# A four-layer graph network on one core: GRU states through a DRAM scratch and VectorE block transposes, with a new order of steps

## What is computed

```python
x = _layernorm(x + _L0_gnn_ref(x, adj, ...))     # attention, 4 heads: "pre"
x = _layernorm(x + _L1_gnn_ref(x, adj, ...))     # 3 GRU turns: "gru"
x = _layernorm(x + _L2_gnn_ref(x, L2_adj, adj, ...))  # relations: "rel"
x = _layernorm(x + _L3_gnn_ref(x, adj, ...))     # attention, 1 head: "post"

# _L1_gnn_ref
for i in range(3):
    m = jnp.einsum('bnd,de->bne', h, weight[i])
    aggr = jnp.einsum('bst,bsd->btd', A, m)
    h = _gru_cell(aggr, h, w_ih, w_hh, b_ih, b_hh)
```

## Time and profile before

| | |
|---|---|
| median of 3 runs | 2612.03 us (2610.0 to 2612.58) |
| profiled execution | 2609.57 us, of which the span 2607.8 |
| granted TensorE clock, mean | 0.991 |
| TensorE busy | 2514.1 us, 96% |
| VectorE busy | 1962.8 us, 75% |
| ScalarE busy | 1779.6 us, 68% |
| GpSimd busy | 1240.7 us, 48% |
| DMA | 198.51 MB, 611560 packets |

### The profile page before, as it was taken

One profiled execution on the slowest core, in us unless ns is written; L12 is line 12 of the kernel. 1 busy time (PEld: TensorE's weight loads), 2 busy tenths in 40 slices (PEclk: granted clock), 3 DMA queues, 4 the chain that ended last, 5 costly groups with the idle time before them and its releaser, 6 DMA issues. The chain is left out here.

```text
span 2607.8 us, 48430 instructions
## 1 busy us (share of the span) xinstructions
PE 2514.1 (96%) x14379; PEld 2158.4 (83%) x14379; DVE 1962.8 (75%) x4883; ACT 1779.6 (68%) x4536; POOL 1240.7 (48%) x1584
## 2 busy tenths in 40 slices
PE   7999999999999999999999999999999999999985
PEld 6888888888888888888888888888888888888874
DVE  7867777777777777777777777777777777787653
ACT  6556776676776676776676776676776676776654
POOL 1344555554554544554554554444555454455442
PEclk9999999999999999999999999999999999999996
DMA  5222333333333333333333233333333333233200
GB/s 152 83 50 69 78 91 73 78 80 78 72 92 72 81 76 85 70 88 76 79 75 89 68 86 77 78 75 82 75 84 80 76 78 86 68 84 76 49 14 23
DMA packets 611560, 198.51 MB, mean 76 GB/s; under 512 B 456768, under 2 KB 596288, under 8 KB 611264
## 3 DMA queue, kind: packets, MB, share of 16 engines
q1 hardware_dynamic: 559472, 146.54, 26.2%
q10 hardware_dynamic: 51792, 48.38, 5.5%
HBM read 146.81 MB, written 48.01 MB: 75 GB/s over the span
## 5 line engine op out<-in xcount | busy, mean ns | idle before, releaser
L988 PE MATMUL psum<-ag_h,wc_h 128*128 128x512 f32 (+1 forms) x1188 | 489.3, 412 | 5.5 <-DVE ag_l L1519 3.5
L988 PE MATMUL psum<-ht_h,whh_h 128*128 128x512 f32 (+1 forms) x1188 | 476.9, 401 | 1.4 <-ACT g_z L1220 1.4
L988 PE MATMUL psum<-ht_h,whh_l 128*128 128x512 f32 (+1 forms) x1188 | 461.9, 389 | 0.0
L988 PE MATMUL psum<-ht_l,whh_h 128*128 128x512 f32 (+1 forms) x1188 | 461.9, 389 | 0.0
L988 PE MATMUL psum<-ag_h,wc_l 128*128 128x512 f32 (+1 forms) x1188 | 461.6, 389 | 0.0
L988 PE MATMUL psum<-ag_l,wc_h 128*128 128x512 f32 (+1 forms) x1188 | 461.3, 388 | 0.0
L1643 POOL TENSOR_TENSOR ht<-ht,g_n 128x512 f32<-128x512 f32 (+1 forms) x198 | 264.6, 1336 | 252.0 <-ACT g_n L1225 251.8
L1592 POOL TENSOR_SCALAR rstd<-moments 128x2 f32<-128x2 f32 x256 | 66.5, 260 | 664.7 <-DVE moments L1444 657.1
L988 PEld LDWEIGHTS psum<-ag_h,wc_h 128*128 128x128 f32 x1188 | 224.2, 189 | 57.2 <-DVE ag_l L1519 15.7
L988 PEld LDWEIGHTS psum<-ht_h,whh_l 128*128 128x128 f32 x1188 | 223.8, 188 | 50.5
L988 PEld LDWEIGHTS psum<-ag_h,wc_l 128*128 128x128 f32 x1188 | 223.5, 188 | 50.2
(11 more groups left out here) (150 smaller groups left out, 6123.0 us busy)
## 6 DMA issues: line engine op xcount, KB each, us to landing
x_kept<-x ACTq DMA_DIRECT2D x118, 256.0 KB, 2.2
x_blocks<-x_kept SPq DMA_DIRECT2D x472, 64.0 KB, 2.4
first_scores<-first_kept SPq DMA_DIRECT2D x116, 256.0 KB, 3.5
adj_i<-in_adj_dram SPq DMA_DIRECT2D x128, 128.0 KB, 3.3
x_in<-in_x_dram SPq DMA_DIRECT2D x64, 256.0 KB, 4.1
out_dram<-out_t ACTq DMA_DIRECT2D x64, 256.0 KB, 2.3
x_blocks<-in_x_dram SPq DMA_DIRECT2D x232, 64.0 KB, 3.4
part<-in_adj_dram SPq DMA_DIRECT2D x32, 256.0 KB, 3.3
```

The lines of the kernel that those rows point to most:

```text
L988: last = mm(dst, s, m, start=(first and k == 0), stop=(last_part and k == len(flat) - 1))
```

## The change

The states of layers 0 and 1 of halves 2 to 29 no longer go through TensorE and ScalarE on their way to hn. A new step h_keep, in ScalarE's queue, stores the new state in two DMAs to a DRAM scratch (two of them in turn); a new step h_blocks, in SP's queue, loads one unit of it in four DMAs into the ring xs; gru_turn is then one block transpose of 128x512 on VectorE. For the other halves (0, 1, 30 and later) gru_turn stays as it was. GpSimd's gru_n, the first to overwrite ht in the next turn, waits for the store. The table HALF is written anew: it has the new steps, and others have other places.

```diff
+    "h_blocks": ("xs",),
-    "gru_agg": ("light",), "gru_turn": ("light",), "gru_fin": ("light", "yf"),
+    "gru_agg": ("light",), "gru_fin": ("light", "yf"),
...
+def h_blocked(k):
+    return H_BLOCKED <= k < H_LAST
...
@@ the table HALF @@
-gru_in(0,0,0)  att_low(post,-2,0)  dve.gru_in(0,0,0)  gru_new(-1,1,1)  gru_split(-1,1)
+gru_in(0,0,0)  gru_new(-1,1,1)  att_low(post,-2,0)  att_xt(pre,1,1)  gru_split(-1,1)  att_rows(post,-2,0)
+        h_blocks(-1,1,1)
...
+H_BLOCKED = 2
+H_LAST = 30
...
+            def h_blocks(k, l, hf):
+                i = take(sp, "xs", "h_blocks", k, l, hf)
+                slot_of, landed = kept_state(k, l)
+                sp.wait_ge(s_h_kept[slot_of], landed)
+                blocks = h_kept[slot_of][hf].rearrange("c (f b) (q n a) -> n b q (c f) a", b=TURN, q=2, a=TURN)
+                for n in range(P // TURN):
+                    sp.dma_start(xs[i][n * TURN:(n + 1) * TURN].rearrange("b q (m a) -> b q m a", a=TURN), blocks[n]).then_inc(s_xs[i], 16)
...
@@ TensorE, gru_agg @@
-                    pe.wait_ge(s_nd, turned_back(k, l - 1, 0 if k else 1) + len(units(k)) - 1)
+                    pe.wait_ge(s_ndb if h_blocked(k) else s_nd, turned_back(k, l - 1, 0 if k else 1) + len(units(k)) - 1)
...
@@ TensorE and ScalarE @@
             def gru_turn(k, l, hf):
+                if h_blocked(k):
+                    return
...
@@ ScalarE's queue @@
+            def h_keep(k, l):
+                n = KEPT.index((k, l))
+                act.wait_ge(s_hnew, half_of_turn(k, l, 1))
+                if n >= 2:
+                    act.wait_ge(s_ndb, turned_back(*KEPT[n - 2], 1))
+                for hf in range(2):
+                    act.dma_start(h_kept[n % 2][hf].rearrange("c p n -> p c n"), ht[k % 2][:, :, 2 * hf * P:(2 * hf + 2) * P]).then_inc(s_h_kept[n % 2], 16)
...
@@ VectorE @@
+            def gru_turn(k, l, hf):
+                if not h_blocked(k):
+                    return
+                i, rounds = ring("xs", "h_blocks", k, l, hf)
+                if hf == 0:
+                    take(dve, "nodes", "gru_turn", k, l, hf)
+                dve.wait_ge(s_xs[i], 64 * (rounds + 1))
+                stand(dve)
+                nc.vector.transpose(hn[:, 2 * hf:2 * hf + 2, :], xs[i][:]).then_inc(s_ndb, 1)
...
@@ GpSimd, gru_n @@
+                if l > 0 and c == 0 and h_blocked(k):
+                    slot_of, landed = kept_state(k, l - 1)
+                    pool.wait_ge(s_h_kept[slot_of], landed)
```

More of the change, by code:

```diff
@@ L102 @@
[L102 to L106, removed]
-gru_agg(-1,2,1)  att_pt(post,-2,0,0)  att_scores(pre,1,1,0)
[L108 to L129, removed]
@@ L130 @@
-gru_rzh(0,1,1)  rel_h1(-1,0)
-gru_r(0,1,1)  x1_turn(1,1)  gru_new(0,1,0)  att_pt(post,-2,1,0)  att_rows(pre,2,0)  pe.gru_z(0,1,1)  act.x1_turn(1,1)
-        att_wh(pre,2,0,0)  att_wh(pre,2,0,1)  gru_norm(-1,1)  rel_y1(-1,0)  att_pv(post,-2,1)  rel_rest(-1,0)
+x1_low(0,1)
+gru_z(-1,1,1)  act.x1_turn(0,1)  att_spread(pre,1,0,0)  att_exp(post,-3,1)  rel_norm(-2,0)  x3_keep(-2,0)
+        att_res(post,-3,1)  dve.att_res(post,-3,1)
+gru_agg(0,0,0)
+gru_agg(0,0,1)
+gru_in(-1,1,1)  att_scores(pre,1,0,0)  rel_bias(-2,1)  att_scores(pre,1,0,1)  att_spread(pre,1,0,1)
@@ new lines @@
+gru_hn(0,0,0)  gru_n(-1,1,1)  pre_load(1,1)  x3_blocks(-2,0)  sp.att_rows(post,-2,0)  act.gru_hn(0,0,0)
+        h_blocks(-1,1,0)  att_spread(post,-2,0,0)
+gru_rzh(0,0,0)
+gru_r(0,0,0)  att_prob(pre,1,0)  rel_mask(-2,1)  act.att_xt(post,-2,0)
+gru_z(0,0,0)  att_xt(post,-2,0)  rel_adjt(-2,1)  dve.att_xt(post,-2,0)
+gru_in(0,0,0)  gru_new(-1,1,1)  att_low(post,-2,0)  att_xt(pre,1,1)  gru_split(-1,1)  att_rows(post,-2,0)
+        h_blocks(-1,1,1)
+gru_hn(0,0,1)  att_pt(pre,1,0,0)  h_keep(-1,1)  pool.gru_split(-1,1)  dve.gru_split(-1,1)  att_pt(pre,1,0,1)
+        dve.gru_in(0,0,0)  rel_h1(-2,1)  att_wh(post,-2,0,0)  att_wh(post,-2,0,1)  act.att_xt(pre,1,1)
+        act.rel_h1(-2,1)  gru_n(0,0,0)
@@ new lines @@
+gru_rzh(0,0,1)  att_low(pre,1,1)  act.gru_n(0,0,0)  att_pv(pre,1,0)  act.att_pt(pre,1,0,1)  gru_new(0,0,0)
+        att_rows(pre,1,1)  dve.rel_y1(-2,1)  att_wh(pre,1,1,0)  att_wh(pre,1,1,1)  att_exp(pre,1,0)  gru_turn(-1,1,0)
+        rel_y1(-2,1)  rel_rest(-2,1)  att_norm(post,-3,1)  dve.att_scores(post,-2,0,0)  act.att_scores(post,-2,0,0)
+        dve.gru_turn(-1,1,0)  dve.gru_z(0,0,1)  dve.gru_turn(-1,1,1)
+gru_r(0,0,1)
+gru_z(0,0,1)  att_spread(pre,1,1,0)  att_scores(post,-2,0,0)  sp.pre_load(2,0)  gru_turn(-1,1,1)  att_store(post,-3,1)
+        att_prob(post,-2,0)  x3_blocks(-2,1)
@@ new lines @@
+gru_in(0,0,1)  dve.att_res(pre,1,0)  att_res(pre,1,0)  rel_norm(-2,1)  att_spread(pre,1,1,1)  x3_keep(-2,1)
+        gru_n(0,0,1)
+gru_hn(-1,2,0)
+gru_agg(-1,2,0)
+gru_agg(-1,2,1)  att_pt(post,-2,0,0)  att_scores(pre,1,1,0)
+gru_rzh(-1,2,0)  act.gru_r(-1,2,0)  gru_new(0,0,1)  h_keep(0,0)  pool.gru_n(0,0,1)  att_exp(post,-2,0)
+        act.att_xt(post,-2,1)  pre_load(2,0)  att_pv(post,-2,0)  gru_split(0,0)  att_xt(post,-2,1)
+        pool.gru_split(0,0)
+gru_r(-1,2,0)  h_blocks(0,0,0)
+gru_z(-1,2,0)  att_low(post,-2,1)  dve.gru_in(-1,2,0)  att_scores(pre,1,1,1)  act.gru_z(-1,2,0)
+        act.att_scores(pre,1,1,1)  h_blocks(0,0,1)  x_blocks(2,0)  att_prob(pre,1,1)
@@ new lines @@
+gru_in(-1,2,0)  dve.att_res(post,-2,0)
+gru_hn(-1,2,1)  gru_turn(0,0,0)
+gru_rzh(-1,2,1)  gru_n(-1,2,0)  att_wh(post,-2,1,0)  act.gru_turn(0,0,1)  dve.att_pt(post,-2,0,0)  gru_turn(0,0,1)
+        pool.gru_n(-1,2,1)  att_res(post,-2,0)
+gru_r(-1,2,1)  gru_load(1)  att_wh(post,-2,1,1)  att_rows(post,-2,1)  att_pt(pre,1,1,0)  att_norm(pre,1,0)
+        dve.gru_z(-1,2,1)
+gru_z(-1,2,1)  dve.att_pt(pre,1,1,1)  att_pt(pre,1,1,1)  x1_keep(1,0)  gru_new(-1,2,0)  post_load(-1,0)
+gru_in(-1,2,1)  x1_blocks(1,0)
@@ new lines @@
+gru_in(0,1,0)  dve.x1_turn(1,0)  pool.gru_fin(-1,1)  dve.gru_in(0,1,0)  att_scores(post,-2,1,0)  dve.gru_fin(-1,1)
+        gru_fin(-1,1)  att_low(pre,2,0)  gru_norm(-1,0)
+gru_hn(0,1,1)  att_prob(post,-2,1)
+gru_rzh(0,1,1)  gru_n(0,1,0)  x1_low(1,0)  att_norm(post,-2,0)  act.gru_n(0,1,0)  att_store(post,-2,0)
+        pool.rel_rest(-1,0)  x1_blocks(1,1)  x_blocks(2,1)  rel_h1(-1,0)
+gru_r(0,1,1)  x1_turn(1,1)  sp.att_rows(pre,2,0)  gru_new(0,1,0)  att_pt(post,-2,1,0)  act.gru_r(0,1,1)
+        att_rows(pre,2,0)  gru_norm(-1,1)  dve.rel_y1(-1,0)  att_wh(pre,2,0,0)  att_wh(pre,2,0,1)  rel_y1(-1,0)
+        pe.gru_z(0,1,1)  att_pv(post,-2,1)  rel_rest(-1,0)
```

48 lines of the change are left out of this document (28 added, 20 removed).

## The result

The kernel after took 2659.7 us (median of four runs, 2656.44 to 2660.32), the kernel before 2611.0 beside it: a ratio of 1.0186 (interval 1.0173 to 1.0198). The forecast was 2548, the range ended at 2594.

What follows compares the result with a forecast made beforehand. TensorE was taken as the bound, busy 2168.56 of 2200 us in the steady part. 2609.57 less 50 (transposes) and 14 (idle) gives 2545.6, with 2.5 for the runs' median 2548 us; 8-in-10 range 2526 to 2594.

Steps and rivals of the forecast that it cites:

- What leaves TensorE: On TensorE in halves 2 to 29: 448 transposes go, in 112 calls of gru_turn at 0.45 us, saving 50 us.
- Half of the idle goes: TensorE's 31.4 us idle in the steady part: half counted as gone after new small waits, -14 us (-31 to 0).
- The moved steps: New order in HALF: TensorE reaches gru_agg(-1,2,0) at 29.9 us of the half, not 28.96; two regular waits shrink.
- The chain of state (-1,1): Blocks to gru_agg(-1,2,0) through SP and VectorE: slack between 1.5 us and nothing, a wait of 0.1 to 0.2 us taken.
- That of (0,0): Store, loads and transposes ahead of gru_agg(0,1,0): more room, second transpose ends about 2 us before it.
- other waits that come from the reordered steps alone: Listed sign on the whole kernel that would show the forecast wrong; no size given.
- Rival (c): DRAM path becomes the limit ahead of gru_agg(-1,2,0): 2.4 to 3.9 us wait per half, 2629 to 2671 us; chance 0.08.

Runs made afterwards that it cites:

- e14: The order of e12, but VectorE transposes the states where they lie, with no store or load; 2559.8 us, ratio 0.9807 to the kernel before.
- e12: Kernel after with three moves undone (rel_norm with x3_keep, gru_load(1), rel_h1(-2,1)) and TensorE turning all states; 2609.0 us, ratio 0.9993 to before.
- e6: e1 without store and loads: order of before, gru_hn(-1,2,0) moved, VectorE transposes the state where it lies; 2604.1 us, ratio 0.9972 to before.
- e2: Kernel after's order alone: no half is blocked, TensorE turns and ScalarE copies all states; 2643.5 us, ratio 1.0123 to before.
- e9: Kernel after without store and loads: VectorE transposes the state where it lies; 2617.3 us, ratio 1.0028 to before.
- e1: The path alone: order of before with the new steps put in and gru_hn(-1,2,0) ahead of gru_agg(-1,2,0); 2668.0 us, ratio 1.0217 to before.
- e13: e5 with only gru_load(1) moved: SP loads adj_g behind layer 0's blocks, GpSimd makes the edges later; 2596.8 us, ratio 0.9953 to before.
- e4: Kernel after with one move undone: gru_load(1) again ahead of pre_load(2,0); 2661.9 us, ratio 1.0209 to before.
- e5: Kernel after, path kept, with three moves undone (rel_norm with x3_keep, gru_load(1), rel_h1(-2,1)); 2661.3 us, ratio 1.0181 to before.
- e7: e1 with TensorE and ScalarE turning the states as before; store and loads run, their blocks read by nobody; 2637.8 us, ratio 1.0099 to before.

## Why the prediction was wrong, point by point

- **"What leaves TensorE" (-50 us)** was sized rightly: the work of a half fell by 1.6 to 1.8 us in every kernel without the transposes, and e14 against e12 is 49 us. The step that failed is that this time lies on the path. In the order of before it filled the wait for xt_l; 7 of 50 came through (e6). In the new order it filled the one of rel_h1(-1,0); 26 of 50 came through (e2 to e9). The earlier trace rows counts only the wait that is left, not the one that is covered; the starts of the earlier trace rows gave the price of a call, and I did not ask whether the operand behind it was ready.
- **"Half of the idle goes" (-14 us)** had the wrong sign. xt_l went as argued (29.4 to 8.8 us), but the gaps rose from 1.9 to 5.4 us per half. first_scores was to shrink as well and rose from 10.9 to 19.5, because att_scores(pre,1,0,*) came 1.8 us later on ScalarE (6.99 us of the half instead of 5.21), more than the 1.4 by which TensorE's own place was to move. ScalarE in the half of before that starts at 1236.74, then in the one of after that starts at 1258.80:

```profile
1239.91 1.10 ACT L1237 ACTIVATE x<-y_t,shift,rstd 128x256 f32<-128x256 f32 x2 [1.43 <-POOL shift L1597]
1241.95 0.39 ACT L1136 ACTIVATE first_scores<-first_scores,wh 128x128 f32<-128x128 f32 x1
```

```profile
1263.22 1.09 ACT L1290 ACTIVATE x<-y_t,shift,rstd 128x256 f32<-128x256 f32 x2 [2.42 <-POOL shift L1660]
1264.82 1.09 ACT L1247 ACTIVATE ag_h<-psum 128x512 fp32r<-128x512 f32 x2 [0.50 <-ACT x L1290]
1265.79 0.40 ACT L1179 ACTIVATE first_scores<-first_scores,wh 128x128 f32<-128x128 f32 x1
```

att_scores stands behind rel_norm (x) in both. rel_norm starts 1.25 us later in the half (4.42 instead of 3.17), since GpSimd's shift comes later, at the end of a chain that begins with rel_h1(-1,0) in the half before; and two ag_h instead of one now stand between, 0.5 us.
- **The moved steps** were walked only where they touch the state's chain. rel_norm and x3_keep ahead of gru_agg's ag_h, rel_h1 ahead of att_wh, and gru_load on GpSimd were not, and together they are the whole +32 of the order (with all three undone e2's 2643.5 becomes e12's 2609). The list of what would show it wrong named "other waits that come from the reordered steps alone"; nothing in the sum carried them.
- **The chain of state (-1,1)** had the right mechanism: in every half of after from 420 to 2080 us gru_agg(-1,2,0) starts 0.1 to 0.2 us after the second transpose. The forecast wait was 0.1 to 0.2 us, the measured one 0.46. That it came so near is partly luck: the two ends that were compared, 30.0 and 29.9 us of the half, came at 32.2 and 32.3, both late by the same waits ahead of them. **That of (0,0)** was put at 2 us of room, and TensorE waits there too, 0.26 us per half. The store's landing was taken at 2.2 us from the earlier trace rows, the median of x_kept over all places; in after it is 3.1 us in the mean at this place, and where the loads of the next unit leave beside it, as in e1, it is 5.2.
- **Rival (c)** holds the measured time (2629 to 2671), but by luck: it has the path cost 2.4 to 3.9 us of wait for hn per half, and after waits under 1 us for it, while 32 of the 49 us are the order's. It had the block loads landing late for state (-1,1); their median is 2.4 us in before and after alike. What can land late is the store, above all for the other state. It was given 0.08 since the DMA engines are busy 0.34 of the time, a mean over places of the half that move from 0.1 to 1.4 MB in 8 us; the 1.4 is where layer 0's store was to leave. The Trainium skill, "DMA: Bandwidth & Descriptors", warns of latency under load and of small pieces. On latency the runs agree (2.5 against 5.2 us for the store of e1 at its two places). On small pieces no run can decide, since none has other pieces; the loads of the states, in pieces of 128 bytes, landed after 2.4 and 2.7 us in the mean at their two places in after, 3.9 at most.
- **Why the change as a whole is +49**: order +32; path in it -26 by the turns (e9 against e2) and +42 by the transfers (after against e9).

What stays open: e13 against e14 leaves 37 us to the transfers even with the store well placed; the gaps that show are first_turned (0.40 us per half) and hn (0.25), the rest is spread, and it wasn't split further. Which of the order's three moves costs how much without the path wasn't run either. Some VectorE instructions are stretched: 28 of after's 75 of one form of 128x512 (first_scores, median 0.69 us) take more, up to 1.81 us. That alone isn't the cause: all such excess between 500 and 2000 us is 39 us on VectorE in before, 53 in after, and 63 in e14, the fastest kernel here.

## What to carry to other kernels

Before counting removed TensorE work as gain, look at the first instruction behind each removed piece and at when its operand is ready: a piece that ends just as the operand arrives is the filler of a hidden wait. Price a transfer by the landing of what leaves at that same place in the loop, not by its median, and keep the store that somebody waits for clear of prefetches, which can be issued behind it. Where a change moves steps, walk each on each engine: each of three harmless-looking moves put an operand late, and undoing only one or two left the time where other waits held it.

## What was not expected of the hardware

A single wait of TensorE for hn of 1.2 to 2.6 us was accompanied or followed, in 11 of 36 halves of e4 and e5, by a granted clock of 0.50 for 7 to 10 us, and such a half took 81.4 to 83.7 us instead of 78 to 79. Waits up to 2.2 us also passed without it. Behind waits for xt_l and g_r e1 has 3.4 us at 0.50 in 5 of 21 halves, and 24 us in all between 200 and 2400 us, against 3.4 in e7; it is part of its 37 us, by an estimate (half of that time lost) at most 10. The Trainium skill, "TensorE: Matmul & The Clock Gate", Part 1, describes a gate that sets the clock by how busy the array was of late; these rows agree with that much.
